# Middle stages of a graph network by groups of tiles: expert rows, division with scatter, type rows as bf16 terms, two norms staggered

## The reference, cut to what matters

```
x = x + L0_gnn(LN(x))   msgs = edge_weight*x[src]; h = (1+eps)*x + segment_sum(msgs, dst)
                        h = relu(h@w1 + b1)@w2 + b2
x = x + L0_ffn(LN(x))   8 experts, top 1, 1024 hidden; y = nan_to_num(ybuf[idx,pos]*prob*kept)
x = x + L1_gnn(LN(x))   K,Q,V = typed_linear(x); two passes over the edges (col and row):
                        att = seg_softmax(k.q); agg += segment_sum(v*att), e0 beside it
                        o = typed_linear([agg,agg], Wa, ba)      # Wa is (19, 512, 256)
                        y = o + LN(x); yn = norm(y); return yn*gamma[type] + beta[type]
x = x + L1_ffn(LN(x))   slice attention: softmax over 64 slices in 8 heads, tokens, output
```

## Time and profile before

| | us |
|---|---|
| median of three runs | 4485.64 |
| the profiled execution | 4489.73 |
| its span | 4488.0 |
| PE busy / DVE busy / POOL busy / ACT busy | 2749.5 / 2543.2 / 2727.8 / 1624.9 |

### The profile page before, as it was taken

The page is one execution under the profiler, slowest core; times in us unless marked ns, Lnnn a source line. Parts: engine busy times, 40 slices in busy tenths (PEclk is TensorE's granted clock), DMA queues, the critical chain, the costliest instruction groups (busy, mean ns, idle before and its releaser), DMA issues.

```text
span 4488.0 us, 57931 instructions
## 1 busy us (share of the span) xinstructions
PE 2749.5 (61%) x13804; PEld 1878.1 (42%) x13804; DVE 2543.2 (57%) x5123; ACT 1624.9 (36%) x4283; POOL 2727.8 (61%) x2589
## 2 busy tenths in 40 slices
PE   3200005555555782067777869886777878876598
PEld 1000004333453451023444447774444457765346
DVE  7645545555440003434999975557999955552753
ACT  1111100000021110013666657775666657763031
POOL 3777777777677776846777734446777724446100
PEclk6555557777787896588999989998999989997598
DMA  8333349333433544387999955557899945554000
GB/s 338 145 141 141 137 133 256 105 105 105 102 125 108 208 155 145 67 225 230 276 276 275 275 140 143 141 143 212 273 271 272 257 111 142 140 131 128 13 1 29
DMA packets 763466, 742.24 MB, mean 165 GB/s; under 512 B 385207, under 2 KB 650639, under 8 KB 763232
## 3 DMA queue, kind: packets, MB, share of 16 engines
q1 hardware_dynamic: 640820, 395.52, 30.7%
q0 software_dynamic: 115760, 316.99, 23.9%
q10 hardware_dynamic: 6672, 27.26, 1.5%
HBM read 481.29 MB, written 267.14 MB: 167 GB/s over the span
## 4 chain that ended last, share of the span: by engine, by line
DVE 23%; PE 21%; issue 19%; POOL 10%; DVEq 7%; DMA 4%; SPq 2%; ACT 1%; POOLq 0%; ACTq 0%
DVE BIGR L1244 11%; POOL AR L1467 6%; PE ps L575 5%; DVE AR L1264 5%; DVEq L1260 4%; PE ps L870 3%; PE ps L879 3%; POOL rec_src L462 2%; DVE BIGR L555 1%; DMA AR<-typ_x 1%; PE ps L2047 1%; PE ps L1846 1%; PE ps L1853 1%; DVE AR L546 1%; DMA BIGR<-in_L_ffn_w 1%
## 5 line engine op out<-in xcount | busy, mean ns | idle before, releaser
L1220 POOL DMA_INDIRECT AR<-kv_tab,META x832 | 792.4, 952 | 270.2 <-issue 252.1
L1467 POOL TENSOR_TENSOR AR<-AR 128x896 f32<-128x896 f32 x208 | 351.2, 1688 | 522.1 <-ACT AR L1527 522.1
L437 POOL DMA_INDIRECT rec_dst<-AR,slot_e x400 | 441.4, 1103 | 185.6 <-issue 121.7
L1444 DVE TENSOR_TENSOR BIGR<-BIGR,ps 128x260 f32 x832 | 353.5, 425 | 303.9 <-PE ps L1500 155.2
L1244 DVE TENSOR_REDUCE BIGR<-ps 128x8 f32<-128x1024 f32 x416 | 507.5, 1221 | 16.4 <-PE ps L1353 1.1
L462 POOL DMA_INDIRECT rec_src<-AR,slot_e x400 | 422.3, 1056 | 125.3 <-issue 121.7
L575 PE MATMUL ps<-AR 128*128 128x256 f32 x832 | 303.9, 530 | 289.2 <-issue 198.6
L529 POOL DMA_INDIRECT AR<-xn_tab,META x416 | 397.2, 955 | 132.6 <-issue 121.6
L1500 PE MATMUL ps<-AR 128*128 128x260 f32 x1664 | 426.2, 400 | 80.0 <-POOL AR L1467 70.3
L575 PEld LDWEIGHTS ps<-AR 128*128 128x128 f32 x832 | 210.7, 265 | 383.0 <-issue 323.4
L1500 PEld LDWEIGHTS ps<-AR 128*128 128x128 f32 x1664 | 298.7, 191 | 170.4 <-DVE BIGR L1444 127.1
(11 more groups left out here) (409 smaller groups left out, 5818.1 us busy)
## 6 DMA issues: line engine op xcount, KB each, us to landing
v_dst<-AR SPq DMA_DIRECT2D x104, 384.0 KB, 4.1
AR<-v_dst SPq DMA_DIRECT2D x104, 384.0 KB, 3.5
v_src<-AR SPq DMA_DIRECT2D x104, 384.0 KB, 4.9
AR<-v_src SPq DMA_DIRECT2D x104, 384.0 KB, 3.5
AR<-in_W_qvk SPq DMA_DIRECT2D x44, 608.0 KB
rec_dst<-BIGR ACTq DMA_DIRECT2D x1, 26624.0 KB, 90.3
rec_raw<-AR SPq DMA_DIRECT2D x40, 640.0 KB, 3.0
AR<-rec_raw POOLq DMA_DIRECT2D x40, 640.0 KB, 4.3
```

The source lines that it names most:

```text
L437: pool.indirect_dma_start(rec_tab[0], bass.IndirectOffsetOnAxis(ap=slot_e[0][:, c * CC + k:c * CC + k + 1].bitcast(U32), axis=0), RD[s][0] ...
L1220: pool.indirect_dma_start(KVR[s][:, u, 0:KV], None, kv_tab, bass.IndirectOffsetOnAxis(ap=META[o][:, g * U + u, 0:1].bitcast(U32), axis=0)) ...
L1444: ve.tensor_tensor(a, a, PS[4 + u][:, 0:SROW], ALU.add).then_inc(sem("add"), 1)
L1467: pool.tensor_tensor(v, v, VB[s][:, :, D:SROW].unsqueeze(3).to_broadcast([P, U, H1, DK]), ALU.mult).then_inc(sem("pv"), 1)
```

## The change

By parts, with the names of the code:

1. **MLP**: DVE forms the head one tile ahead (`head(step + 1)`), three buffers `HS` instead of two.
2. **`rec_src`**: chunks 0 to 6, 7 to 31 and 32 to 34 stand at the three old places. The last five chunks (50 indirect DMAs) are issued by POOL in the sum pass o = 0, one behind the weighing of each of the first 50 groups; SP loads their records before. The `META[1]` columns are loaded in the same pass, in four pieces at groups 62, 70, 78 and 86.
3. **Wa**: DVE adds the halves beside the experts, three types at a time (seven 128x1536 sums). SP loads both halves there.
4. **Expert rows**: 25 gathers in groups of 4, 7, 7 and 7 tiles (`XGRP`), the gate on ACT, repair and sum on DVE in seven subgroups of up to four tiles, statistics behind each, the norm per group on ACT; the scatters to `typ_x` wait per group.
5. **End of a sum pass**: o = 0 divides straight into `AGG`; o = 1 divides and adds by the four groups, and the scatters wait per group.
6. **Type rows**: `ba`, `beta` and `gamma` are split into three bf16 terms that stand on three times 32 partitions under a tripled one-hot in bf16. Their products stand between the steps of the projection.
7. **Last norms**: rows of y come back by groups, and the norm of y and that of x run staggered by groups: statistics on DVE, scaling and normalising on ACT. The slices start behind the last group.

```diff
-            for step in range(N2 + 2):
-                t = step
-                if t < N2:
-                    if t >= 2: ve.wait_ge(sem("mlp_ht"), t - 1)
-                    ve.scalar_tensor_tensor(out=HS[t % 2], ...)
+            head(0)
+            for step in range(N2 + 2):
+                if step + 1 < N2:
+                    head(step + 1)
...
         def expert_rows_pool(pool):
-            for t in range(NT):
-                pool.indirect_dma_start(YG[:, t, :], None, moe_out, ...).then_inc(sem("moe_rows"), 16)
+            for k in range(4):
+                for t in range(XGRP[k], XGRP[k + 1]):
+                    pool.indirect_dma_start(YG[:, t, :], None, moe_out, ...).then_inc(sem(f"rows{k}"), 16)
...
         def expert_rows_vector(ve):
+            for a, b in XSUB:
+                ve.wait_ge(sem("gated"), b)
+                ve.tensor_scalar(BAD[:, 0:n], y, 0.0, 0.0, ALU.mult, ALU.not_equal)
+                ve.tensor_scalar(REP[:, 0:n], y, FMAX, None, ALU.is_gt)
+                ve.scalar_tensor_tensor(out=REP[:, 0:n], in0=y, scalar=-FMAX, in1=REP[:, 0:n], ...)
+                ve.tensor_scalar(REP[:, 0:n], REP[:, 0:n], -10000.0, None, ALU.mult)
+                ve.copy_predicated(y, BAD[:, 0:n], REP[:, 0:n])
+                ins = ve.tensor_tensor(x, x, y, ALU.add)
+                for t in range(a, b):
+                    ve.bn_stats(bst[:, t % 2, :], X[:, t, :])
+                    ve.bn_aggr(mv[:, t, :], bst[:, t % 2, :])
...
         def experts_vector(ve):
+                if e:
+                    ve.wait_ge(sem("ex_out"), 16 * e)
+                    ve.wait_ge(sem("wa_in"), 32 * (e + 1))
+                    ve.tensor_tensor(WSR[:, t0:t0 + n, :], WSR[:, t0:t0 + n, :], WLOW[:, 0:n, :], ALU.add)
...
         def sum_pool(pool, o):
+            pool.wait_ge(sem("tail_in"), 16 * (NCK - CL))
+            for g in range(NG):
+                weigh(g // SL, g % SL)
+                if g < CC * (NCK - CL):
+                    pool.indirect_dma_start(rec_tab[1], ..., R2T[c - CL][:, k * REC:(k + 1) * REC], ...)
...
         def sum_vector(ve, o):
-                ve.tensor_tensor(AGG, AGG, ACC[:, :, 0:D], ALU.add).then_inc(sem("agg"), 1)
+                for k in range(4):
+                    for h in range(H1):
+                        ve.tensor_tensor(a, a, RCP[:, sl, h].unsqueeze(2).to_broadcast([P, n, DK]), ALU.mult)
+                    ve.tensor_tensor(AGG[:, sl, :], AGG[:, sl, :], ACC[:, sl, 0:D], ALU.add).then_inc(sem("agg"), 1)
...
         def proj_scalar(act):
+            for q in range(4):
+                act.wait_ge(sem("prep_ps"), 2 + q + 1)
+                act.activation(OHT[:, a:b], OHP4[q][:, 0:b - a], ACT.Copy).then_inc(sem("oht"), 1)
+            act.wait_ge(sem("agg"), 4)
             for t in range(25):
                 act.activation(XT3[:, t, :], X[:, t, :], ACT.Identity, ...).then_inc(sem("xt3"), 1)
...
+        def norm_vector(ve):
+            sums(0)
+            sums(1)
+            scale(0)
+            sums(2)
+            scale(1)
+            residual(0)
+            sums(3)
+            scale(2)
+            residual(1)
+            final(0)
+            scale(3)
+            residual(2)
+            final(1)
+            residual(3)
+            final(2)
+            final(3)
```

More of the change, by code:

```diff
@@ new lines, in expert_rows_scalar, with normal, roots @@
+        def expert_rows_scalar(act):
+            def normal(k):
+                act.wait_ge(sem("nmr"), k + 1)
+                for t in range(XGRP[k], XGRP[k + 1]):
+                    act.activation(XNI[:, t, 0:D], X[:, t, :], ACT.Identity, scale=rs[:, 3, t:t + 1], bias=nmr[:, t:t + 1]
+                                   ).then_inc(sem("xn"), 1)
+            def roots(k):
+                sl = slice(XGRP[k], XGRP[k + 1])
+                act.wait_ge(sem("var"), VAR3 + k + 1)
+                act.activation(rs[:, 1, sl], rs[:, 0, sl], ACT.Sqrt).then_inc(sem("sd"), 1)
+            for k in range(4):
+                act.wait_ge(sem(f"rows{k}"), 64 * (NG // SL) + 16 * (XGRP[k + 1] - XGRP[k]))
+                for t in range(XGRP[k], XGRP[k + 1]):
+                    act.activation(YG[:, t, :], YG[:, t, :], ACT.Identity, scale=gate_p[:, t:t + 1]).then_inc(sem("gated"), 1)
+                if k >= 2:
+                    roots(k - 2)
+                    normal(k - 2)
+            for k in range(2, 4):
+                roots(k)
+                normal(k)
@@ L953, in expert_rows_vector @@
+                ve.drain()
+                if due is not None:
+                    normal(due)
+                    due = None
+                if b in XGRP:
+                    due = XGRP.index(b) - 1
+                    sl = slice(XGRP[due], b)
+                    ve.tensor_scalar(rs[:, 0, sl], mv[:, sl, 1], LN_EPS, None, ALU.add).then_inc(sem("var"), 1)
+            normal(due)
             ve.drain()
@@ L1204, in score_sync @@
                     load(g + 3)
-        ROWS0 = 64 * (NG // SL)
+        ROWS0 = [64 * (NG // SL) + 16 * (XGRP[s + 1] - XGRP[s]) for s in range(SL)]
         def score_pool(pool, o):
@@ L1597, in project @@
                 ins.then_inc(sem("tile_mm"), 1)
-            pe.wait_ge(sem("wa_sum"), len(NWA))
+            pe.wait_ge(sem("wa_sum"), len(WAR))
+            pe.wait_ge(sem("oht"), 4)
+            pe.wait_ge(sem("late"), late("gb3"))
+            rows(pe, 0)
+            rows(pe, 1)
             turn(0)
@@ L1665, in proj_vector @@
+            for k in range(3):
+                ins = ve.tensor_tensor(OH3[:, :, 32 * k:32 * k + 32], iotaz[:, 0:32].unsqueeze(1).to_broadcast([P, NT, 32]),
+                                       NTY2[:, :].unsqueeze(2).to_broadcast([P, NT, 32]), ALU.is_equal)
+            ins.then_inc(sem("late"), 1)
+            split3(ve, GBT, GB1, GBB, STK[0:ST], GB3).then_inc(sem("late"), 1)
             for t in range(25):
@@ L1669, in proj_vector @@
                 ve.tensor_tensor(X[:, t, :], X[:, t, :], PS[6 + t % 2][:, 0:D], ALU.add).then_inc(sem("pre"), 1)
-            ve.drain()
-            for t in range(25):
-                if t % 6 == 0 and t < 24:
-                    ve.wait_ge(sem(f"y_rows{t // 6}"), 16 if t < 18 else 32)
-                ve.tensor_tensor(YN[:, t, :], YN[:, t, :], XT3[:, t, :], ALU.add)
-                ve.drain()
-                ve.bn_stats(YST[:, t % 2, :], YN[:, t, :])
-                ve.drain()
-                ve.bn_aggr(YMV[:, t, :], YST[:, t % 2, :])
```

522 lines of the change are left out of this document (313 added, 209 removed).

## The result

The changed kernel took 4293.32 us (median of four runs, 4291.52 to 4297.36), the kernel before 4483.45 in the same setting: a ratio of 0.9574, with a 95% interval of 0.9553 to 0.9596. The forecast was 4316, with a range of 4278 to 4385. The profiled execution took 4297.4 us, its span is 4295.2 against 4488.0, so 192.8 us are to be found.

| stretch | before | after | difference | forecast |
|---|---|---|---|---|
| start to the first row scatter (MLP, routing) | 1345.9 | 1305.0 | -40.9 | -33 |
| to the first expert gather | 372.5 | 383.1 | +10.6 | +6 |
| to the first key product (the middle) | 220.2 | 112.9 | -107.2 | -103 |
| to the first weighing of the first sum pass | 732.7 | 735.4 | +2.7 | 0 |
| to the first gather of the second score pass | 384.2 | 380.2 | -4.0 | +5 |

A forecast was written before the change was run, and what follows sets the result against it. No engine was taken to hold the span, so stages were read singly: MLP -33, experts +6, middle -103, first sum pass +5, end -47, sum -172, giving 4318 from 4489.7; forecast 4316, range 4278 to 4385.

The forecast's parts named there:

- 20 steps of 1.31: MLP: PE's 1.31 us wait for the head goes in 20 steps outside the seams, giving 26 us.
- the seams: MLP: at four seams of five tiles the wait is 4.97 us; one head in store saves 7 to 8 in all.
- 2 us for each of three waits: Experts: low halves of Wa ahead of three pairs' loads lengthen PE's waits at pair starts, +6 in all.
- the 8 taken: Middle: POOL's indirect DMAs lose 8 us beside DVE's passes; ends 0 and 29.
- the 5 taken: Middle: from the end of the last typed scatter to PE, 4 to 5 us, taken as 5.
- The rival of 29 lost: Middle: DVE's passes hold POOL for all of 29 us, +21, total 4339; chance 0.12.
- costs of 3 and 5: First sum pass: +3 for scatters behind 50 weighings, +5 for column loads sharing DMA engines.
- a gain of 3 for the copy that goes: First sum pass: the copy into AGG at the pass's end goes, -3.
- the pass pays: First sum pass: added work costs time; half price +30 to 40, 4350, all of it 4402; chance 0.13.
- the slow one: First sum pass: DVE's sums hold the 50 scatters, 273 us, total 4591; chance 0.04.
- the estimate: End: four copies of turned one-hots, ahead of ACT's projection copies, put at 4058 to 4062.
- The sign of being wrong that the prediction named: End: wrong if ACT's copies rather than POOL's scatters set the projection's start by more than 10 us.

The follow-up runs named there:

- the second experiment: The changed kernel with the last five chunks of scatters (50) back on POOL behind the expert rows, against the changed kernel: 4359.20 us, ratio 0.9722.

## Why the prediction was right

- **Chain by seams.** No engine was the bound, and each stretch was summed by what waited last. Every term came within 9 us, and 172 us forecast stand against 192.8 found between the spans. Six of the eight stretches gained more than forecast; the experts and the key products lost more.
- **MLP.** The mechanism was right and the size too small: -33 forecast, -40.9 found. The term "20 steps of 1.31" took the step less its wait, 2.77 us; it became 2.59, 1.49 less than 4.08. That is 29.8, and the seams gave 11 instead of 7. With the order alone undone, all of it is gone (115.4 us from first to last head product, as before).
- **Experts.** +6 forecast, +10.6 found. The term took 2 us for each of three waits; they grew by 3.7, 3.2 and 4.1, which is all of it. So 2.3 us of transfer at the best rate of a slice were too small a price, if the low halves are the cause. On chip A 10 to 11 us come back when the low halves are moved.
- **Middle.** -103 and -107.2. The sum over POOL's own row was right in each part: 102.8 us of DMAs, 6.7 lost to DVE for the 8 taken, 3.5 us from the last typed scatter's end to PE for the 5 taken. The rival of 29 lost would have needed long passes: seven-tile passes already lose 9 more. Of the 107 us, 68 are shown to be the scatters' by the second experiment; the other 40 (the sums of Wa, the work by groups, the edge columns out of the way) were not taken back one by one.
- **First sum pass.** +5 forecast, -4.0 found. The sum took costs of 3 and 5 and a gain of 3 for the copy that goes. Of the costs some 2 us were there at most by the second experiment. The gain was not there: from the last weighing to the next pass's first gather 4.62 us pass before and 4.65 after, since POOL does not wait for DVE's division. The 4 us that went lie between the first and the last weighing, and their reason was not found. So the mechanism (PE binds, the scatters fit in POOL's gaps) was right, and that the sum stayed near is in part luck. The rival "the pass pays" and the slow one (scatters held by DVE) fall: scatters take 1.00 us there.
- **End.** -47 and -48.5. ACT's first copy came at +50.2 us from the last sum where the sum had 47.0: its copies of one-hots ended at +38.0, and the estimate had +34.5 at the latest. The sign of being wrong that the prediction named, ACT and not POOL setting the start, is there with 3.1 us, not with 10; in the kernel where ACT copies the x rows first, the first y scatter comes 4.8 us earlier. The projection took 64.1 for 64.4 us and the norm chain 66.0 for 66.3. The 4.5 us for PE at its low clock behind the norms had no row, and no run shows them alone: from the norm's start to the third softmax 89.2 us passed where the sum had 92. Of the rows of types, bf16 took off 15 us and left DVE as their bound; their place between the steps hid the rest.
- **Not forecast.** -4.6 us in the last 200 us: PE's last 200 products take 43.41 us instead of 45.90, with a granted clock of 1.00 instead of 0.94 over them; the other 2.1 lie in the 151 us ahead, with 0.95 instead of 0.93. +2.7 in the key products stays open.
- **The range.** The prediction calls 4286 and 4402 the full ends of its terms. 4286 is right; all dear ends together (-8, +12, -80, +89, -35) give 4468, and 4402 is the dear end of the first sum pass alone. The measured time does not touch that side.

## What to carry to other kernels

Work of a queue that has a gap in every step of a long, differently bound pass is almost free there and costs its full length in a serial seam: 50 scatters took 68 us in one place and some 2, if anything, in the other. Where one engine waits for a value that another could have made earlier in its written order, change that order first; nothing else was needed in the MLP. Beside GpSimd's indirect DMAs, keep DVE's passes short: seven-tile passes lost 9.2 us more than four-tile ones over 80 DMAs. And let a kernel to compare with run in each set: one and the same kernel took 4486 us on one chip and 5302 on another.

## What the runs showed of the hardware that was not expected

On the second kind of chip PE issued one product every 2.80 us for long stretches while POOL's scatters ran beside the experts, then none for 85 us, and reached its usual pace only when they had ended. PE's timeline of the changed kernel there (chip B), and DVE's with a copy of a finished product:

```profile
1652.30 0.58 PE L899 MATMUL ps<-BIGR 128*128 128x256 f32 x1 [2.21 <-issue]
1655.10 0.58 PE L899 MATMUL ps<-BIGR 128*128 128x256 f32 x1 [2.22 <-issue]
...
1711.11 0.37 PE L882 MATMUL ps<-ident,AR 128*128 128x128 f32 x1 [2.44 <-issue]
1796.61 6.56 PE L890 MATMUL ps<-AR,BIGR 128*128 128x512 f32 x8 [85.13 <-issue]
...
1774.12 0.42 DVE L937 COPY AR<-ps 128x256 f32<-128x256 f32 x1 [47.17 <-issue]
```

and windows around 1832.61 us, where POOL's last scatter starts:

```profile
1700.00:1800.00 100.00, 5.15 (x9) 2.23 (x9) 3.21 (x4) 0.60 (x1) 69.55 (x74) 0.50 0.28 94
1800.00:1836.00 36.00, 13.95 (x19) 4.87 (x18) 0.00 (x0) 2.75 (x4) 25.97 (x28) 0.69 0.26 83
1836.00:1900.00 64.00, 47.52 (x149) 28.25 (x148) 4.48 (x7) 8.94 (x15) 0.00 (x0) 0.84 0.30 103
```

Nine products in 100 us with 74 scatters beside them, 149 in 64 us with none. "issue" says that no semaphore or transfer in the profile held the engine, and DVE is held like PE. The kernel with four chunks fewer there had its first gather 45 us earlier, and its scatters ended 55.7 us earlier (each from the first row scatter). On the first kind of chip the same code runs 245 products in 100 us beside 81 scatters (1346 to 1446 us, PE busy for 77.30). In the first sum pass, with one scatter each 3.7 us, the second kind shows nothing of it (375.5 to 378.8 us).

This is not all that differs. Of the 766 us by which the changed kernel's span is longer on chip B, 283 lie in the expert stage, 148 ahead of it (the MLP's head products take 149.8 us for 74.8), and 162 and 158 in the stretches of the two score passes (897.5 us for 735.4, and 1128.8 for 970.7 with the second sum pass). There the granted clock is lower (0.75 instead of 0.96 in the second score pass), and the bf16 products of L1400 take 487 ns on the mean instead of 392. What holds back the issue beside the scatters, what lowers the clock in the score passes, and why one chip has it and another not, is open.
